# A local-attention stage on one core: per-head norms inverted by Newton steps on VectorE instead of a square root on ScalarE, with a new table of step times

## The reference, cut to what matters

```python
for i in range(DEPTH):                                   # 6
    x = attn_layer(shift_tokens(x), Wqkv[i], ...) + x
    x = ffn_layer(shift_tokens(x), ln_g[i], ...) + x
# attn_layer: 16 heads of 64, windows of 32 tokens, each looks at itself and the window before
q = l2norm(q) * qs;  k = l2norm(k) * ksc                 # t / max(norm(t), 1e-12)
q = q*cos*scale + rotate_half(q)*sin*scale               # k with 1/scale
sim = einsum(q, k2) * 8;  attn = softmax(masked sim);  out = attn @ v2 @ Wo
# ffn_layer
xn = (x - mu) / sqrt(var + 1e-05) * g + bln
a, gate = split(xn @ W1 + b1);  return a * gelu(gate) @ W2 + b2
```

## Time and profile before

| | us |
|---|---|
| three runs | 5428.46, 5443.51, 5441.09 |
| median | 5441.09 |
| the profiled execution, its own time | 5428.46 |
| its span | 5427.0 |

### The profile page before, as it was taken

How to read it: one execution, slowest core, us unless ns; L and a number is a source line. 1 busy time by engine, 2 the same in 40 slices (tenths; PEclk the granted TensorE clock), 3 DMA queues, 4 the chain that set the end, 5 groups by cost and what they waited for, 6 DMA issues and landing times. The chain is left out here.

```text
span 5427.0 us, 142807 instructions
## 1 busy us (share of the span) xinstructions
PE 4945.6 (91%) x59480; PEld 2993.1 (55%) x59480; DVE 4415.0 (81%) x9246; ACT 3591.0 (66%) x6391; POOL 2895.9 (53%) x3375
## 2 busy tenths in 40 slices
PE   5999996999999999999999999999986999978978
PEld 2333333666666666666666666666643555544445
DVE  5899995988888888988888889889944777767655
ACT  1777885777777777777777777777741667645522
POOL 1221002878877877787778777877731111024634
PEclk6999998999999999999999999999985999988989
DMA  0000002000000000000000000000000000000000
GB/s 22 1 1 1 1 1 70 14 8 12 25 14 10 10 25 14 10 10 25 13 10 10 25 14 15 10 10 14 4 3 24 2 2 2 2 15 1 1 1 16
DMA packets 46743, 63.26 MB, mean 12 GB/s; under 512 B 11260, under 2 KB 33602, under 8 KB 45202
## 3 DMA queue, kind: packets, MB, share of 16 engines
q1 hardware_dynamic: 46098, 54.14, 3.3%
HBM read 25.17 MB, written 4.19 MB: 5 GB/s over the span
## 5 line engine op out<-in xcount | busy, mean ns | idle before, releaser
L939 PE MATMUL psum<-b_w_qk,b_xst 128*128 128x512 f32 x1536 | 808.8, 609 | 11.1 <-DVE b_cross L1220 9.8
L1369 POOL TENSOR_TENSOR x<-x,b_norm 128x512 f32<-128x512 f32 x576 | 593.2, 1044 | 407.8 <-DVE b_norm L1236 407.8
L1015 PE MATMUL psum<-b_w_vo,b_mixed 128*128 128x128 f32 x6144 | 797.2, 278 | 3.5 <-ACT b_mixed L1116 3.3
L1015 PEld LDWEIGHTS psum<-b_w_vo,b_mixed 128*128 128x128 f32 x6144 | 736.9, 192 | 67.3 <-issue 50.2
L587 DVE TENSOR_REDUCE a_top<-psum 128x1 f32<-128x512 f32 x1024 | 637.6, 683 | 89.4 <-PE psum L434 87.5
L537 ACT ACTIVATE a_prob<-psum 128x512 f32<-128x512 f32 x1024 | 556.4, 601 | 136.0 <-PE psum L450 127.9
L1086 ACT ACTIVATE x<-psum 128x512 f32<-128x512 f32 x768 | 465.4, 606 | 156.4 <-DVE b_norm L1228 144.7
L1228 DVE TENSOR_REDUCE b_norm<-x 128x8 f32<-128x512 f32 x768 | 514.0, 672 | 67.2 <-ACT x L1086 63.7
L1116 ACT COPY b_mixed<-psum 128x512 f32<-128x512 f32 x768 | 411.0, 587 | 238.0 <-PE psum L1000 238.0
L1220 DVE TENSOR_TENSOR b_cross<-psum,b_table 128x512 f32<-128x512 f32 x768 | 522.5, 680 | 0.0
L587 DVE TENSOR_REDUCE c_top<-psum 128x1 f32<-128x512 f32 (+3 forms) x768 | 384.2, 552 | 156.2 <-PE psum L434 153.8
(11 more groups left out here) (314 smaller groups left out, 11135.0 us busy)
## 6 DMA issues: line engine op xcount, KB each, us to landing
b_prev<-b_xs_x SPq DMA_DIRECT2D x24, 384.0 KB
b_w_qk<-in_L_ffn_Wqkv SPq DMA_DIRECT2D x6, 1024.0 KB, 7.2
b_shifted_x<-y SPq DMA_DIRECT2D x24, 224.0 KB, 2.5
b_shifted_f<-y SPq DMA_DIRECT2D x24, 224.0 KB, 2.5
b_w_v<-in_L_ffn_Wqkv SPq DMA_DIRECT2D x6, 512.0 KB, 7.4
b_w_o<-in_L_ffn_Wo SPq DMA_DIRECT2D x6, 512.0 KB, 9.2
b_prev<-b_xs_x SPq DMA_DIRECT2D x24, 112.0 KB
x<-in_L_attn_x SPq DMA_DIRECT2D x4, 512.0 KB, 5.9
```

Source lines behind the costliest of these rows:

```text
L939: e.matmul(banks[n], xst_of(l, b)[:, P * t:P * (t + 1)], w_qk[l % 2][:, BANK * c:BANK * (c + 1)], start=True, stop=True).then_inc(filled[n ...
L1015: made = e.matmul(banks[n][:, 0:D], mixed[:, h, :], w_vo[l % 2][:, h, :], start=h == 0, stop=h == 2 * PAIRS - 1)
L1369: e.tensor_tensor(rh, rh, bcast(norm[i % 2][:, 1, HPC * c:HPC * (c + 1)], 2, LDIM), ALU.mult).then_inc(sem["scaled"], 1)
```

## The change

There are three parts. **The inverse of the norms** no longer uses ScalarE's square root. It becomes nine steps: a maximum with 1e-24 on the sums of squares, a first guess of `1/sqrt` made by integer arithmetic on the bits, and two refinement steps, in each of which ScalarE squares the guess and VectorE does the rest. Seven of the nine are VectorE's, on 128x32 elements, two are ScalarE's (`Square`). A factor of the refinement is folded into the rotary tables on the host. **The layer norm** gets the same treatment with three Newton steps: after epsilon come the guess, and three times a square on ScalarE and two operations on VectorE. The last product of the layer norm stays. The buffers with 1e-12 go. **The tables of times** are new, and the scores of a tile are issued in one step instead of two.

```diff
-FF_BEGINS, FF_SLOTS, NORM_PARTS, LAST_PROJECT = 12, 3, 2 * TILES + 4, 3
+FF_BEGINS, FF_SLOTS, NORM_PARTS, LAST_PROJECT = 12, 3, 2 * TILES + 12, 3
 PIECES = dict(
...
-    sum_squares=(9.27, 11.10, 12.03, 15.20), add=(12.65, 13.99, 17.94, 20.17), invert=(14.94, 17.16, 17.32),
+    sum_squares=(9.59, 15.58, 15.75, 15.90), add=(13.90, 14.09, 15.81, 19.25), invert=(16.64, 16.71, 17.29, 17.99, 18.20, 18.56, 20.40, 20.60, 20.84),
...
 # score on TensorE
-                    for m in (step[2], 2 + step[2]):
+                    for m in range(4):
...
-                    for p in range(4 * step[2], 4 * step[2] + 4):
+                    for p in range(PAIRS):
...
 # invert on ScalarE
-                if kind == "invert" and step[2] == 0:
-                    q.wait_ge(sem["summed"], all_of("sum_squares", i))
-                    q.wait_ge(sem["inverted"], INVERT_PARTS * i)
-                    e.activation(bounded[i % 2][:, :, 0], norm[i % 2][:, 0, :], ACT.Sqrt).then_inc(sem["inverted"], 1)
+                if kind == "invert" and step[2] in (2, 5):
+                    q.wait_ge(sem["inverted"], INVERT_PARTS * i + step[2])
+                    e.activation(norm[i % 2][:, 2, :], norm[i % 2][:, 1, :], ACT.Square).then_inc(sem["inverted"], 1)
...
 # norm on ScalarE
-                    e.activation(chip.spread[:, k % 2, :, 0], chip.mean_var[:, k % 2, :, 1],
-                                 ACT.Sqrt).then_inc(sem["norm_parts"], 1)
+                    e.activation(chip.spread[:, k % 2, :, 0], chip.spread[:, k % 2, :, 1],
+                                 ACT.Square).then_inc(sem["norm_parts"], 1)
...
 # invert on VectorE
-                    if step[2] == 1:
-                        made = e.tensor_reduce(nm[:, 0, :], bounded[i % 2][:, :, :], AX.X, ALU.max)
+                    if part == 0:
+                        made = e.scalar_tensor_tensor(out=squares, in0=squares, scalar=1e-24, in1=squares, op0=ALU.max, op1=ALU.max)
+                    elif part == 1:
+                        made = e.tensor_scalar(root.bitcast(I32), squares.bitcast(I32), -0.5, float(0x5f1ffff9), ALU.mult, ALU.add)
+                    elif part == 3:
+                        made = e.scalar_tensor_tensor(out=tmp, in0=tmp, scalar=-1.0, in1=squares, op0=ALU.mult, op1=ALU.mult)
+                    elif part == 4:
+                        made = e.scalar_tensor_tensor(out=root, in0=tmp, scalar=2.38924456, in1=root, op0=ALU.add, op1=ALU.mult)
+                    elif part == 6:
+                        made = e.scalar_tensor_tensor(out=tmp, in0=tmp, scalar=FIRST_STEP * FIRST_STEP, in1=squares,
+                                                      op0=ALU.mult, op1=ALU.mult)
+                    elif part == 7:
+                        made = e.scalar_tensor_tensor(out=squares, in0=tmp, scalar=-10.0 / 3.0, in1=tmp, op0=ALU.add, op1=ALU.mult)
                     else:
-                        made = e.reciprocal(nm[:, 1, :], nm[:, 0, :])
+                        made = e.scalar_tensor_tensor(out=root, in0=squares, scalar=5.0, in1=root, op0=ALU.add, op1=ALU.mult)
```

More of the change, by code:

```diff
@@ L42 @@
 QK_SCALE = 8.0
+FIRST_STEP = 0.703952253
 WPT = P // WINDOW
@@ L705 @@
 PIECES = dict(
-    project=(-0.02, 2.74, 8.92, 11.78), square=(2.41, 7.84, 10.76, 12.81), rope=(4.23, 10.44, 11.41, 15.62),
-    sum_squares=(9.27, 11.10, 12.03, 15.20), add=(12.65, 13.99, 17.94, 20.17), invert=(14.94, 17.16, 17.32),
-    scale=(19.10, 19.10, 20.57, 26.31), turn=(18.96, 22.74, 24.33, 29.08), copy_turned=(20.83, 22.40, 26.53, 30.10),
-    score=(30.19, 33.37), top=(33.89, 34.97), less=(34.99, 35.74), exp=(34.06, 36.34),
-    sum=(36.07, 36.88), invert_sum=(36.27, 36.99), weigh=(36.51, 36.91), block=(37.82, 40.61),
-    gather=(42.91,), spread=(42.72, 42.49, 43.36, 47.43), out=(49.27, 50.84, 52.64, 53.00), join=(56.06,))
+    project=(0.00, 3.34, 7.97, 14.01), square=(1.73, 3.79, 12.67, 15.75), rope=(6.06, 11.25, 15.71, 17.74),
+    sum_squares=(9.59, 15.58, 15.75, 15.90), add=(13.90, 14.09, 15.81, 19.25), invert=(16.64, 16.71, 17.29, 17.99, 18.20, 18.56, 20.40, 20.60, 20.84),
+    scale=(23.17, 25.84, 25.49, 21.55), turn=(23.50, 26.17, 27.21, 30.16), copy_turned=(24.20, 29.34, 31.52, 30.81),
+    score=(33.08,), top=(36.19, 35.98), less=(37.43, 37.49), exp=(38.90, 39.16),
+    sum=(39.25, 41.08), invert_sum=(40.26, 41.54), weigh=(42.06, 45.10), block=(44.49, 46.34),
+    gather=(46.96,), spread=(47.71, 47.96, 47.46, 49.15), out=(49.54, 51.94, 53.60, 55.45), join=(62.15,))
 INVERT_PARTS = len(PIECES["invert"])
-NORM_ROOT = 2 * TILES + 1
-FF_PIECES = dict(fill=(14.63, 20.66, 24.59), empty=(16.52, 21.90, 24.93))
+NORM_SQUARES = range(2 * TILES + 2, NORM_PARTS - 1, 3)
+FF_PIECES = dict(fill=(16.45, 21.44, 26.66), empty=(18.74, 24.10, 29.55))
 def local_order():
@@ L796, in local_stage @@
                 slot["gather", step[1], w] = 4 + w, chip.fills[4 + w]
-        elif kind == "score" and step[2] == 0:
+        elif kind == "score":
             for odd in range(2):
@@ L835, in local_stage @@
         cross = [sb(f"cross{n}", [BANK])[:, :] for n in range(3)]
-        norm = [sb(f"norm{n}", [2, 2 * LHEADS]) for n in range(2)]
-        bounded = [sb(f"bounded{n}", [2 * LHEADS, 2]) for n in range(2)]
+        norm = [sb(f"norm{n}", [3, 2 * LHEADS]) for n in range(2)]
         xs_x, prev = ([sb(f"{label}{n}", [TILES, D]) for n in range(2)] for label in ("xs_x", "prev"))
@@ L1229, in vector_ @@
                                     ALU.add).then_inc(sem["summed"], 1)
-                if kind == "invert" and step[2] > 0:
-                    nm = norm[i % 2]
-                    q.wait_ge(sem["inverted"], INVERT_PARTS * i + step[2])
-                    if step[2] == 1:
-                        made = e.tensor_reduce(nm[:, 0, :], bounded[i % 2][:, :, :], AX.X, ALU.max)
+                if kind == "invert" and step[2] not in (2, 5):
+                    part, nm = step[2], norm[i % 2]
+                    squares, root, tmp = (nm[:, m, :] for m in range(3))
+                    q.wait_ge(sem["summed"], all_of("sum_squares", i))
+                    q.wait_ge(sem["inverted"], INVERT_PARTS * i + part)
+                    if part == 0:
[11 more added lines that the diff above has]
+                        made = e.scalar_tensor_tensor(out=squares, in0=tmp, scalar=-10.0 / 3.0, in1=tmp, op0=ALU.add, op1=ALU.mult)
                     else:
-                        made = e.reciprocal(nm[:, 1, :], nm[:, 0, :])
+                        made = e.scalar_tensor_tensor(out=root, in0=squares, scalar=5.0, in1=root, op0=ALU.add, op1=ALU.mult)
                     made.then_inc(sem["inverted"], 1)
@@ L1295, in vector_ @@
                                       banks[n].rearrange("p (a d) -> p a d", a=4)).then_inc(emptied[n], 1)
-                if kind == "norm" and step[3] != NORM_ROOT:
+                if kind == "norm" and step[3] not in NORM_SQUARES:
                     l, b, part = step[1:]
```

21 lines of the change are left out of this document (12 added, 9 removed).

## The result

The changed kernel took 5692.55 us (median of four runs, 5682.57 to 5700.12), the kernel before 5442.3 beside it: ratio 1.0465, 95% interval 1.0438 to 1.049. That is +250 us where +70 was forecast, in the direction forecast and outside the range. The profiled execution has a span of 5683.9 us.

A forecast was written before the change was run, and what follows sets the result against it. TensorE was taken to bound ordinary local-stage tiles, VectorE or hand-overs three in eight. Per eight tiles +2.9 us made 67 us, the first tiles 3; together +70 against the 5441.09 median: 5511 us, range 5465 to 5570.

The forecast's parts named there:

- The scores in one piece: Attention scores of a local-stage tile, issued in one step: claimed to cost TensorE nothing, the instructions being the same.
- The ring: Loop of TensorE's `gather` and scores and VectorE's work up to `block`: 0.7 us slack where VectorE empties no bank.
- rival 3: Much slower: VectorE's work serial with TensorE's, all of 173 + 24 us plus half the bias, 5663 us; chance 0.10.
- The inverse, seven operations at 0.20 us, net +0.9: VectorE, every local-stage tile: seven short operations replace two, net +0.9 us per tile, 173 us over 192; upper bound +1.3.
- Bias tile +1.9: GpSimd's bias addition now delays three `scale` and both `weigh`: +1.9 us in that tile, once in eight.
- Norm tile +1.9: Layer-norm tile, once in eight: 1.9 us of added VectorE work, all put on the path.
- Gelu, -1.2: Gelu tile of the second half: Gelu moves behind both exponentials and clears the path, credited 1.2 us.
- ScalarE in the stage: Sign that the forecast is right: ScalarE busy about 1930 us in the local stage.
- some 100 loads: Sign that the forecast is right: some 100 ScalarE table loads in the program.
- VectorE's stage total: Sign that the forecast is right: VectorE busy about 2960 us in the local stage, +190.
- The sum: Norm, bias, Gelu and ordinary-tile terms added per eight local-stage tiles: +2.9 us, 67 us over 23 groups.
- ordinary tiles: The five of eight local-stage tiles without Gelu, norm or bias: TensorE still sets the period, +0.3 us for all five.

## Why the prediction was off, step by step

- **"The scores in one piece cost TensorE nothing: the same instructions."** This is the step that failed. I counted instructions and not how they arrive. The stops inside the scores rose from 6.9 to 91.6 us, and by the tiles a stop costs its own length: some 85 of the 250 us. Joined alone the scores cost 106. The trace of before gave little warning, one stop of 1.99 us among 15 short waits; but nothing in it supported a zero either, as it held no block of that length. The term should have been a range with an open upper end.
- **The ring, "0.7 us of slack".** In the new order there was none: 0.93 us more in the ring cost 111 us net of the stops that it saved, by the estimate above 0.90 us per tile. I had summed the busy times and one 0.4 us for all hand-overs, and had taken rival 3's weight (0.10) from that. In the old order 139 of the 173 us that I counted for the inverse came through, as rival 3 said.
- **The inverse, seven operations at 0.20 us, net +0.9.** In the old order this was right (+0.84 busy). In the new one the starts in the rows above give 0.34, 0.10, 0.21 and 0.64 us for the first four, and the last three took 0.22, 0.22 and 0.11 in the tile behind: 1.84 less 0.52. L1246 alone stands at 0.64 where I put 0.24, because GpSimd's `add` starts beside it. The net is +1.3, the upper bound. The row I had chosen (218 ns) was no guide to that.
- **Bias tile +1.9.** The mechanism was right: in these tiles TensorE waits 1.7 us in the mean for `scale`, before never, and VectorE 0.6 for `weigh`, before 0.4. The size was about half of +3.97, or of +3.50 less the stops. Missing were the lower clock after the stall and the backlog that the norm tile hands over. Moving the bias back gave 57 us, against 44 for 23 times 1.9.
- **Norm tile +1.9.** Measured +3.71, or +2.79 less the stops, at 21.4 us instead of 19 to 20, VectorE busy 20.35 of 20.90 in the tile shown. Taking the layer norm's steps back gave 45 us, which is 1.9 per group and the size of the term; but the whole norm tile also bears L1246, the lock on L1187 (366 ns) and L1183 (493 ns), and TensorE's clock.
- **Gelu, -1.2.** Not seen: +0.49 and +0.12. The exponentials of the second half were freed of their load, and the tile gained nothing by it; what bounds it instead was not looked into.
- **What was right.** ScalarE in the stage 1942 us (1930 forecast); some 100 loads (106 in the program, 91 of them in the two groups above); L1248, L1251, L1253 at 0.18 to 0.19 us; VectorE's stage total +237 against +190, short by what the lock adds: L1246's 0.52 us above L1253, 192 times, is 100 us, and the rest of the additions came to less than counted.

The sum was +2.9 per eight tiles and came to +10.0: stops 3.9 where nothing stood, norm and bias tiles 6.3 instead of 3.8, Gelu +0.1 instead of -1.2, ordinary tiles -0.3 instead of +0.3. Rival 3's price, 5663, was the nearest, but by luck: its cause, VectorE's work serial with TensorE's in every tile, holds in the old order, while in the new one the ordinary tiles less their stops are as long as before. The way was forecast rightly. The norm and bias tiles lost the most, some 150 us, but 87 of them were forecast; of the 7.1 us per eight tiles that the sum missed the stops are the largest part.

**What stays open.** The norm and bias tiles carry some 150 us (126 in 160 tiles), of which both repairs together gave back 62. How the rest divides among the order, the lock, the lower clock and the backlog was not separated. Splitting the scores in the new order was tried in two places, and each made other waits longer, so that the stops were never taken away by themselves. That they come from late instruction packets rests on their coincidence; no run changed how instructions are fetched.

## What to carry to other kernels

Joining blocks of many short matmuls is not free because the instructions stay the same: measure it alone, and look for idle time put down to "issue" inside the block. When a short VectorE operation is placed, look at what GpSimd starts at the same release, not only at the operation's own length. Measure a new order with the old computation and the new computation in the old order, and then compare the waits and not only the times: here 263 and 250 us were lost by waits that are only partly the same. Where tiles differ, compare each with its own place in the pattern, with and without the event in question.
